# Cross attention in steps: turns four steps behind the scores, keys first in a batch, the projection in two pieces

## The chip, the cores and the metric

The kernel runs on one core of one Trainium2 chip. The metric is the device time of one execution in microseconds (us). The engines are PE (TensorE, with its weight loads shown apart as PEld), DVE (VectorE), ACT (ScalarE), POOL (GpSimd), and SP, which here only issues DMAs.

## What is computed

A gated cross attention with a residual, then a gated feed-forward part of attention with experts. Only the first is touched. There are 32 batches of 100 queries and 361 context rows, 256 channels, and 16 heads of 16 channels.

```python
B, S, _ = q.shape                       # 32, 100, 256; k = v = context: 32, 361, 256
Q = jnp.einsum('bsd,ed->bse', q, Wq) + bq
K = jnp.einsum('bsd,ed->bse', k, Wk) + bk
V = jnp.einsum('bsd,ed->bse', v, Wv) + bv
scores = jnp.einsum('bhqd,bhkd->bhqk', Qm, Km) / jnp.sqrt(jnp.float32(Dh))
scores = jnp.where(attn_mask[:, None, :, :], scores, fill)
attn = jax.nn.softmax(scores, axis=-1)
A = jnp.einsum('bhqk,bhkd->bhqd', attn, Vm)
O = jnp.einsum('bsd,ed->bse', A, Wo) + bo
...
x = x + jnp.tanh(g_xattn[0]) * _L0_xattn_ref(_layernorm(x, axis=-1), ctx_1024, ctx_1024, mask_BxSxS2_bf1, ...)
x = x + jnp.tanh(g_ffn[0]) * _L0_ffn_ref(_layernorm(x, axis=-1), ...)
```

## The kernel before

The kernel has a stage for the queries, one for the cross attention (`stage_cross`), and stages for the experts. In the cross attention the batches follow each other, and each batch is 16 steps, one for each head. Every engine has its own program, written out by hand as a loop over the steps (`body(b)`); there is no scheduler. The engines meet at semaphores alone. Batches 0 and 1 and the last four are written out, the others are a hardware loop of two batches an iteration.

In step i of batch b:

- PE multiplies the scores of head i into one of two banks (`p_s`); this needs the maximum of step i-2 to be taken. Then comes a piece of work for another batch, if the table `ahead` or `behind` has one for this step, then `turn`, which transposes the exponentials of an earlier head (three transposes into one of two banks `p_t`), and in every fourth step `attend`, which multiplies four turned heads with the values into `p_a`.
- DVE (`masked`) adds the mask and takes the minimum over the row, which is the (negated) maximum of the softmax, into one of four buffers `sm`. In ten steps of a batch it also copies a turned head from `p_t` to one of eight buffers `ext`.
- ACT takes the exponentials (`exp`) into one of four buffers `ex`, and copies the other six turned heads (`ACT_COPIES`).

`LAG_T`, `LAG_C`, `LAG_E` and `LAG_A` say by how many steps turns, DVE's copies, ACT's copies and attends stand behind the scores; `lagging` carries them over into the next batch.

```python
def lagging(b, i, lag, work):

    if lag <= i < XH + lag:
        work(b, i - lag)
    elif i < lag and not is_first(b):
        work(b.before(), i - lag + XH)
```

Beside that, each batch needs work for its neighbours. The pieces of `keys` and `values` (three matmuls each, into the two banks `p_p`) make the keys of batch b+2 and the values of batch b+1. ACT and DVE split the keys into two halves of 16 bits (`key_hi`, `key_lo`). SP writes them to `k_parts` in DRAM and reads them back stacked as `c_kst`, once the scores of batch b are done (`stack_keys`). ACT copies the values to `vz`. The context is split by POOL (`split`, a CAST and a subtraction) before keys and values can use it; it waits for the values of the batch that used the buffer before. For the batch behind, DVE inverts the denominators (`invert`), POOL spreads them (`spread`), PE turns them (`turn_rden`), ACT copies them (`copy_rt`), DVE multiplies (`normalize`), PE projects (`project_all`), and DVE adds the residual and takes the moments (`residual`, `moments`, `mean_var`); POOL keeps those (`keep`) and SP stores the batch (`store`).

Of the kernel before, what the change touches and what calls it, by code (L numbers as in the profile page):

```python
# [31 lines left out]
DC = D // P  # L32
XH, XD = 16, 16
XG = P // XD
KC = 3
# [59 lines left out]

def is_last(b):
    return isinstance(b.n, int) and b.n == NB - 1


def later(b, n):  # L100

    if isinstance(b.n, int) and b.n + n >= NB:
        return None
    for _ in range(n):
        b = b.next()
    return b
# [219 lines left out]
def stage_cross(nc, k, sems, queries, cross, x, ctx_t, mask, q_parts, k_parts, big, mv, x1):  # L326
# [7 lines left out]

    LAG_T, LAG_C, LAG_E, LAG_A = 3, 4, 3, 5
    RING = 2 * CLOSE
    RT = 256
    ACT_COPIES = (1, 4, 7, 10, 13, 15)  # L340
# [8 lines left out]
    with ExitStack() as ctx:  # L349
# [46 lines left out]
        def sync_programs(sp):  # L396
            def load_ctx(b):
                at_least(sp, s_cl, b.n - 1)
                sp.dma_start(ctxb[:, b.par, :, :],
                             ctx_t[b.n, :, :].rearrange("(c p) s -> p c s", p=P)  # L400
                             ).then_inc(s_ctx[b.par], 16)
# [51 lines left out]
            def body(b):  # L453
                if not is_last(b):
                    n = b.next()
                    load_queries(n)
                    load_rest(n)
                if later(b, 3):
                    load_ctx(later(b, 3))
                if later(b, 2):  # L460
                    stack_keys(later(b, 2))
                if not is_first(b):
                    store(b.before())

            def rest():
                for g in range(4):
                    sp.wait_ge(queries.s_stored[g], 32)
                batches(sp, body)
                store(fixed(NB - 1))
                for par in range(2):  # L470
                    sp.wait_ge(s_st[par], 16 * NB // 2)
# [3 lines left out]
        def gpsimd(pool):  # L475
# [37 lines left out]
            def body(b):  # L513
                if not is_first(b):
                    spread(b.before())
                bias_x(b)
                if later(b, 1):
                    widen_mask(later(b, 1))
                if later(b, 3):
                    split(later(b, 3))  # L520
                if not is_first(b):
                    keep(b.before())

            widen_mask(fixed(0))
            split(fixed(2))
            pool.wait_ge(s_tg, 1)
            batches(pool, body)
            spread(fixed(NB - 1))
            keep(fixed(NB - 1))

        def vector_programs(dve):
# [64 lines left out]
            def start(n):  # L596
# [5 lines left out]
                elif n == 6:  # L602
# [2 lines left out]
                    dve.tensor_scalar(tgbo[:, :], p_p[:, 0, 0:D], k.tanh_g[:, 0:1], None,  # L605
                                      ALU.mult).then_inc(s_tg, 1)

            def body(b):
                for i in range(XH):
                    lagging(b, i, LAG_C, copy_ext)  # L610
                    masked(b, i)
                    if i == 15 and later(b, 2):
                        key_lo(later(b, 2), 0)
                    if i == 0 and not is_first(b) and later(b, 1):
                        key_lo(later(b, 1), 1)
                    if i == 2 and not is_first(b):
                        invert(b.before())
                    if i == 7 and not is_first(b):
                        normalize(b.before())
                    if i == 11 and not is_first(b):  # L620
                        residual(b.before())
                    if i == 12 and not is_first(b):
                        moments(b.before())
                    if i == 13 and not is_first(b):
                        mean_var(b.before())

            def rest():
                batches(dve, body)
# [11 lines left out]
        def scalar_programs(act):  # L640
# [48 lines left out]
            def body(b):  # L689
                for i in range(XH):  # L690
                    lagging(b, i, LAG_E, copy_ext)
                    if i == 15 and later(b, 2):
                        key_hi(later(b, 2), 0)
                    if i == 0 and not is_first(b) and later(b, 1):
                        key_hi(later(b, 1), 1)
                    if i == 6 and not is_first(b):
                        copy_rt(b.before())
                    if i == 4 and not is_last(b):
                        values(b.next(), 0)
                    exp(b, i)  # L700
                    if i in (6, 9) and not is_last(b):
                        values(b.next(), (4, 6, 9).index(i))

            def rest():
                act.wait_ge(queries.s_zero, 3)
# [8 lines left out]
        def tensor_programs(pe):  # L714
            def keys(b, c, kc):
                if kc == 0:
                    if c == 0:
                        pe.wait_ge(s_cl, b.n + 1)
                    at_least(pe, s_vz, KC * b.n - c)
                for i, (w, x) in enumerate(((whi, ctxh), (whi, ctxl), (wlo, ctxh))):  # L720
                    last = pe.matmul(p_p[:, c, 0:SK], w[:, 0, kc, c * P:(c + 1) * P],
                                     x[:, b.par, kc, :], start=kc == 0 and i == 0,
                                     stop=kc == DC - 1 and i == 2)
                if kc == DC - 1:
                    last.then_inc(s_k, 1)

            def values(b, c, kc):
                if kc == 0:
                    if c == KC - 1:
                        pe.wait_ge(s_vz, KC * b.n + 1)  # L730
                    else:
                        pe.wait_ge(s_klo, DC * b.n + c + 1)
                rows = KW if c < KC - 1 else KL
                for i, (x, w) in enumerate(((ctxh, whi), (ctxh, wlo), (ctxl, whi))):
                    last = pe.matmul(p_p[0:rows, c % 2, 0:D], x[:, b.par, kc, c * KW:c * KW + rows],
                                     w[:, 1, kc, :], start=kc == 0 and i == 0,
                                     stop=kc == DC - 1 and i == 2)
                if kc == DC - 1:
                    last.then_inc(s_v, 1)
# [54 lines left out]
                if c == DC - 1:  # L794
                    last.then_inc(s_o, 1)

            def project_all(b):
                for c in range(DC):
                    project(b, c)

            def start(n):
                if n in (0, 3):
                    for m in range(DC * DC):
# [7 lines left out]
                elif n == 5:  # L811
# [3 lines left out]
                    for c in range(DC):  # L815
# [1 line left out]
                    pe.matmul(p_p[:, 0, 0:D], ones[0:1, :], bor[:, :], start=False,  # L817
                              stop=True).then_inc(s_bo, 1)

            ahead = {1: (1, values, 0, 0), 2: (1, values, 0, 1), 3: (1, values, 1, 0), 5: (1, values, 1, 1),  # L820
                     7: (1, values, 2, 0), 9: (1, values, 2, 1),
                     11: (2, keys, 0, 0), 13: (2, keys, 0, 1), 14: (2, keys, 1, 0), 15: (2, keys, 1, 1)}
            behind = {5: (turn_rden,), 10: (project_all,)}

            def body(b):
                for i in range(XH):
                    scores(b, i)
                    if i in ahead and later(b, ahead[i][0]):
                        n, work, *args = ahead[i]
                        work(later(b, n), *args)  # L830
                    if i in behind and not is_first(b):
                        work, *args = behind[i]
                        work(b.before(), *args)
                    lagging(b, i, LAG_T, turn)
                    lagging(b, i, LAG_A, attend)
# [1018 lines left out]
```

## Time and profile before

| | |
|---|---|
| median of 3 runs | 1934.24 us (1933.02 to 1935.41) |
| the profiled execution | 1932.07 us, span 1930.3 us |
| cross attention, first to last exponential | 69.3 to 584.7 us of the span |
| PE busy over the span | 1871.1 us (97%), weight loads 1145.8 us (59%) |
| DVE, ACT, POOL busy | 1476.6 (76%), 1135.5 (59%), 951.1 us (49%) |

The times are those of single executions; the profile is one of them. Matmuls are pipelined, so the busy time of PE counts more than PE's own work. The span holds stages with different limits, so what this change does has to be read from the stretch of the cross attention. Names such as `c_ps` are the kernel's tiles `p_s` and so on, and L746 is a line of the kernel.

### The profile page before, as it was taken

Reading aid. Unit: us, or ns where it says so; the run is one execution under the profiler, and the core shown is the slowest. Engines: PE = TensorE matmul, PEld = TensorE weight load, DVE = VectorE, ACT = ScalarE, POOL = GpSimd, SP = SyncE. Lnnn points to the kernel's source line nnn. Section 1 sums busy time; section 2 is a strip of 40 time slices with the busy share of each in tenths; the row PEclk is TensorE's granted clock in tenths of the full one; section 3 lists DMA queues with packets and bytes.
Section 4 is the critical chain, followed back from the end, with each engine's and each line's share of the span. In section 5 each row is a group of like instructions: output and inputs, shape, how many; then the busy total and the mean of one; then the engine's idle time right before and its main releaser. Section 6 shows DMA issues by size and latency. Waiting matters only on the chain. (4 is left out here: it accounts for less than half of the span.)

```text
span 1930.3 us, 57615 instructions
## 1 busy us (share of the span) xinstructions
PE 1871.1 (97%) x13454; PEld 1145.8 (59%) x13454; DVE 1476.6 (76%) x4245; ACT 1135.5 (59%) x3591; POOL 951.1 (49%) x1432
## 2 busy tenths in 40 slices
PE   5899999999997999999999999999999999999998
PEld 3688888888875555444444445545555555555543
DVE  6688888888887961555555556658999999999989
ACT  3688888888886444444444445545555555555543
POOL 4022222222212001666666666666677676776766
PEclk9999999999998999999999999999999999999999
DMA  6677888788862484000000023122222222222201
GB/s 156 122 118 117 120 119 120 118 120 119 120 88 88 202 329 188 27 27 27 14 27 27 27 82 97 50 71 66 71 80 67 79 75 72 79 70 76 75 15 64
DMA packets 192148, 174.22 MB, mean 90 GB/s; under 512 B 51921, under 2 KB 183378, under 8 KB 190034
## 3 DMA queue, kind: packets, MB, share of 16 engines
q1 hardware_dynamic: 189906, 165.06, 37.7%
q0 software_dynamic: 2176, 8.39, 1.2%
q8 instruction: 28, 0.46, 0.1%
q14 instruction: 38, 0.31, 0.1%
HBM read 112.41 MB, written 60.98 MB: 90 GB/s over the span
## 5 line engine op out<-in xcount | busy, mean ns | idle before, releaser
L1496 POOL TENSOR_TENSOR o_side<-o_side,o_tmp 128x256 f32 (+1 forms) x528 | 397.2, 752 | 195.8 <-POOL o_side L1496 72.8
L1265 PE MATMUL e_pv<-e_vw,e_xhi 128*128 (+1 forms) x1600 | 475.9, 379 | 1.2 <-ACT e_out L1188 1.2
L1198 ACT ACTIVATE big<-e_pv,gates 128x128 f32<-128x128 f32 x800 | 227.9, 368 | 280.8 <-PE e_pv L1265 279.3
L1624 ACT ACTIVATE o_tmp<-o_py,gates 128x256 f32<-128x256 f32 x528 | 221.8, 473 | 193.0 <-PE o_py L1696 143.8
L661 ACT ACTIVATE c_ex<-c_sm,c_nmax 100x361 f32<-100x361 f32 x512 | 302.1, 592 | 53.5 <-DVE c_nmax L554 46.2
L554 DVE CUSTOM_DVE_ANT_0 c_sm<-c_ps,c_mbias 100x361 f32<-100x361 f32 x512 | 267.4, 523 | 55.9 <-PE c_ps L746 51.2
L1696 PE MATMUL o_py<-o_whi,a_chi 128*128 128x512 f16 x800 | 304.2, 380 | 0.1
L1696 PE MATMUL o_py<-o_wlo,a_chi 128*128 128x512 f16 x800 | 303.8, 380 | 0.0
L1696 PE MATMUL o_py<-o_whi,a_clo 128*128 128x512 f16 x800 | 303.7, 380 | 0.0
L1265 PE MATMUL e_pv<-e_vw,e_xlo 128*128 (+1 forms) x800 | 303.2, 379 | 0.0
L1131 DVE TENSOR_SCALAR e_acc<-e_pv,gates 128x128 f32<-128x128 f32 x400 | 121.8, 346 | 227.5 <-PE e_pv L1265 227.4
L1556 DVE SCALAR_TENSOR_TENSOR o_main<-o_py,gates,o_main 128x256 f32 (+1 forms) x536 | 256.1, 478 | 35.4 <-issue 20.2
L1265 PEld LDWEIGHTS e_pv<-e_vw,e_xhi 128*128 (+1 forms) x1600 | 156.5, 98 | 186.6 <-issue 1.6
L1556 DVE SCALAR_TENSOR_TENSOR o_side<-o_py,gates,o_side 128x256 f32 (+1 forms) x536 | 254.1, 474 | 0.1
L753 PE MATMUL c_pt<-ident,c_ex 100*121 100x100 f32 x1536 | 244.1, 268 | 2.7 <-ACT c_ex L661 0.9
L753 PEld LDWEIGHTS c_pt<-ident,c_ex 100*121 100x121 f32 x1536 | 215.8, 185 | 27.0 <-DVE c_ext L564 7.0
L1014 POOL TENSOR_TENSOR big<-big 128x256 f32<-128x256 f32 x200 | 144.8, 724 | 172.2 <-ACT big L1198 124.1
L493 POOL TENSOR_SCALAR c_mbias<-c_mraw 100x361 f32<-100x361 uint8 x32 | 15.9, 497 | 344.3 <-DMA c_mraw<-in_mask 245.8
L746 PE MATMUL c_ps<-c_kst,c_qst 128*100 128x361 f16 x512 | 172.0, 336 | 5.8 <-DVE c_nmax L554 2.2
L564 DVE COPY c_ext<-c_pt 121x300 f32<-121x300 f32 x320 | 148.5, 464 | 9.3 <-PE c_pt L753 7.5
L1607 ACT ACTIVATE a_ex<-a_ps,a_mxs 100x100 f32<-100x100 f32 x256 | 84.5, 342 | 105.1 <-DVE a_mxs L1527 98.5
L1696 PEld LDWEIGHTS o_py<-o_whi,a_clo 128*128 (+1 forms) x800 | 78.2, 98 | 95.1 <-issue 0.8
(164 smaller groups left out, 3206.4 us busy)
## 6 DMA issues: line engine op xcount, KB each, us to landing
qk<-e_out SPq DMA_DIRECT2D x16, 1600.0 KB, 5.2
c_kst<-k_parts SPq DMA_DIRECT2D x256, 90.2 KB, 4.9
a_q<-qk SPq DMA_DIRECT2D x64, 200.0 KB, 2.4
a_k<-qk SPq DMA_DIRECT2D x64, 200.0 KB, 2.4
v<-e_out SPq DMA_DIRECT2D x20, 640.0 KB, 3.3
a_v<-v SPq DMA_DIRECT2D x64, 200.0 KB
c_ctx<-in_ctx_t SPq DMA_DIRECT2D x32, 361.0 KB, 3.4
e_wst<-in_v_w POOLq DMA_DIRECT2D x8, 1024.0 KB, 7.7
```

The source lines that it names most:

```text
L554: dve.tensor_tensor_reduce(out=sm[:, h % 4, :], in0=p_s[0:SQ, h % 2, 0:SK], in1=mbias[:, b.par, :], scale=-0.25 / WS, scalar=BIG, op0=ALU. ...
L564: dve.tensor_copy(ext[:, h % RING, :], p_t[0:KW, h % 2, 0:KC * SQ]).then_inc(s_extd, 1)
L661: act.activation(ex[:, h % 4, 0:SK], sm[:, h % 4, :], ACT.Exp, scale=-1.0, bias=nmax[:, h % 4:h % 4 + 1], accum_out=den[:, b.par, HEAD[h]: ...
L746: pe.matmul(p_s[0:SQ, h % 2, 0:SK], qst[:, b.par, HEAD[h], :], kst[:, b.par, HEAD[h] // 2, :], start=True, stop=True).then_inc(s_s, 1)
L753: last = pe.transpose(p_t[0:KW, h % 2, c * SQ:(c + 1) * SQ], ex[:, h % 4, c * KW:(c + 1) * KW], k.ident[0:SQ, 0:SQ])
L1014: pool.tensor_tensor(tsum[:, hh, :, :], tmp[:, hh, 0:2, :], tmp[:, hh, 2:4, :], ALU.add).then_inc(s_ts, 1)
L1198: act.activation(tmp[:, hh, e, :], p_v[:, hh, 1, e * PD:(e + 1) * PD], ACT.Copy, scale=gate).then_inc(s_av, 1)
L1265: last = pe.matmul(p_v[:, hh, half, :], a[:, c, bass.ds(t * P, P)], vw[:, bass.ds(col + (w * DC + c) * VW, 512)], start=j == 0, stop=j == ...
L1496: pool.tensor_tensor(side[:, x.t, :], side[:, x.t, :], tmp[:, slot(x, r), j, :], ALU.add).then_inc(s_pool, 1)
L1556: dve.scalar_tensor_tensor(out=into[:, x.t, :], in0=p_y[:, q, j, :], scalar=gate, in1=into[:, x.t, :], op0=ALU.mult, op1=ALU.add).then_inc ...
L1624: act.activation(tmp[:, slot(x, r), j, :], p_y[:, q, j, :], ACT.Copy, scale=gate).then_inc(s_av, 1)
L1696: last = pe.matmul(p_y[:, q, :, :].rearrange("p j d -> p (j d)"), a[:, bass.ds(buf * T + x.t * P, P)], b[:, buf, cut], start=j == 0, stop= ...
```

## The change

All four lags grow by one, so turns, copies and attends stand one step further behind the scores. The keys of batch b+2 are made in steps 0, 2, 3 and 4 instead of 11, 13, 14 and 15; the values of batch b+1 in steps 6, 7, 8, 10, 11 and 12 instead of 1, 2, 3, 5, 7 and 9. Attends now stand in steps 1, 5, 9 and 13, where no other piece stands. The projection is split over steps 14 and 15 instead of being whole in step 10, and the residual, moments, `keep` and `store` of a batch follow it, two batches behind, at the start of the next. In the last batch the projection stands in steps 11 and 12. ACT's and DVE's shares of the keys and values move with them.

```diff
--- before.py
+++ after.py
@@ -95,6 +95,10 @@
 
 def is_last(b):
     return isinstance(b.n, int) and b.n == NB - 1
+
+
+def has_two_before(b):
+    return not isinstance(b.n, int) or b.n >= 2
 
 
 def later(b, n):
@@ -334,7 +338,7 @@
 
 
 
-    LAG_T, LAG_C, LAG_E, LAG_A = 3, 4, 3, 5
+    LAG_T, LAG_C, LAG_E, LAG_A = 4, 5, 4, 6
     RING = 2 * CLOSE
     RT = 256
     ACT_COPIES = (1, 4, 7, 10, 13, 15)
@@ -457,15 +461,16 @@
                     load_rest(n)
                 if later(b, 3):
                     load_ctx(later(b, 3))
+                if has_two_before(b):
+                    store(b.before().before())
                 if later(b, 2):
                     stack_keys(later(b, 2))
-                if not is_first(b):
-                    store(b.before())
 
             def rest():
                 for g in range(4):
                     sp.wait_ge(queries.s_stored[g], 32)
                 batches(sp, body)
+                store(fixed(NB - 2))
                 store(fixed(NB - 1))
                 for par in range(2):
                     sp.wait_ge(s_st[par], 16 * NB // 2)
@@ -518,14 +523,15 @@
                     widen_mask(later(b, 1))
                 if later(b, 3):
                     split(later(b, 3))
-                if not is_first(b):
-                    keep(b.before())
+                if has_two_before(b):
+                    keep(b.before().before())
 
             widen_mask(fixed(0))
             split(fixed(2))
             pool.wait_ge(s_tg, 1)
             batches(pool, body)
             spread(fixed(NB - 1))
+            keep(fixed(NB - 2))
             keep(fixed(NB - 1))
 
         def vector_programs(dve):
@@ -605,24 +611,28 @@
                     dve.tensor_scalar(tgbo[:, :], p_p[:, 0, 0:D], k.tanh_g[:, 0:1], None,
                                       ALU.mult).then_inc(s_tg, 1)
 
+            def tail(b, step):
+                if step == 0:
+                    residual(b)
+                if step == 1:
+                    moments(b)
+                if step == 2:
+                    mean_var(b)
+
             def body(b):
                 for i in range(XH):
                     lagging(b, i, LAG_C, copy_ext)
                     masked(b, i)
-                    if i == 15 and later(b, 2):
-                        key_lo(later(b, 2), 0)
-                    if i == 0 and not is_first(b) and later(b, 1):
-                        key_lo(later(b, 1), 1)
+                    if i in (3, 5) and later(b, 2):
+                        key_lo(later(b, 2), i // 5)
                     if i == 2 and not is_first(b):
                         invert(b.before())
-                    if i == 7 and not is_first(b):
+                    if i == 9 and not is_first(b):
                         normalize(b.before())
-                    if i == 11 and not is_first(b):
-                        residual(b.before())
-                    if i == 12 and not is_first(b):
-                        moments(b.before())
-                    if i == 13 and not is_first(b):
-                        mean_var(b.before())
+                    if has_two_before(b):
+                        tail(b.before().before(), i)
+                    if is_last(b):
+                        tail(b.before(), i - 12)
 
             def rest():
                 batches(dve, body)
@@ -689,17 +699,13 @@
             def body(b):
                 for i in range(XH):
                     lagging(b, i, LAG_E, copy_ext)
-                    if i == 15 and later(b, 2):
-                        key_hi(later(b, 2), 0)
-                    if i == 0 and not is_first(b) and later(b, 1):
-                        key_hi(later(b, 1), 1)
-                    if i == 6 and not is_first(b):
+                    if i in (2, 4) and later(b, 2):
+                        key_hi(later(b, 2), i // 4)
+                    if i == 7 and not is_first(b):
                         copy_rt(b.before())
-                    if i == 4 and not is_last(b):
-                        values(b.next(), 0)
+                    if i in (8, 11, 14) and not is_last(b):
+                        values(b.next(), (8, 11, 14).index(i))
                     exp(b, i)
-                    if i in (6, 9) and not is_last(b):
-                        values(b.next(), (4, 6, 9).index(i))
 
             def rest():
                 act.wait_ge(queries.s_zero, 3)
@@ -716,7 +722,8 @@
                 if kc == 0:
                     if c == 0:
                         pe.wait_ge(s_cl, b.n + 1)
-                    at_least(pe, s_vz, KC * b.n - c)
+                    done = b.n if isinstance(b.n, int) and b.n < 2 else b.n - 1
+                    at_least(pe, s_vz, KC * done - c)
                 for i, (w, x) in enumerate(((whi, ctxh), (whi, ctxl), (wlo, ctxh))):
                     last = pe.matmul(p_p[:, c, 0:SK], w[:, 0, kc, c * P:(c + 1) * P],
                                      x[:, b.par, kc, :], start=kc == 0 and i == 0,
@@ -728,8 +735,11 @@
                 if kc == 0:
                     if c == KC - 1:
                         pe.wait_ge(s_vz, KC * b.n + 1)
+                    elif is_last(b):
+                        pe.wait_ge(s_vz, KC * b.n)
                     else:
-                        pe.wait_ge(s_klo, DC * b.n + c + 1)
+                        keyed = b.n if is_first(b) else b.n + 1
+                        pe.wait_ge(s_klo, DC * keyed + c + 1)
                 rows = KW if c < KC - 1 else KL
                 for i, (x, w) in enumerate(((ctxh, whi), (ctxh, wlo), (ctxl, whi))):
                     last = pe.matmul(p_p[0:rows, c % 2, 0:D], x[:, b.par, kc, c * KW:c * KW + rows],
@@ -794,10 +804,6 @@
                 if c == DC - 1:
                     last.then_inc(s_o, 1)
 
-            def project_all(b):
-                for c in range(DC):
-                    project(b, c)
-
             def start(n):
                 if n in (0, 3):
                     for m in range(DC * DC):
@@ -817,10 +823,10 @@
                     pe.matmul(p_p[:, 0, 0:D], ones[0:1, :], bor[:, :], start=False,
                               stop=True).then_inc(s_bo, 1)
 
-            ahead = {1: (1, values, 0, 0), 2: (1, values, 0, 1), 3: (1, values, 1, 0), 5: (1, values, 1, 1),
-                     7: (1, values, 2, 0), 9: (1, values, 2, 1),
-                     11: (2, keys, 0, 0), 13: (2, keys, 0, 1), 14: (2, keys, 1, 0), 15: (2, keys, 1, 1)}
-            behind = {5: (turn_rden,), 10: (project_all,)}
+            ahead = {0: (2, keys, 0, 0), 2: (2, keys, 0, 1), 3: (2, keys, 1, 0), 4: (2, keys, 1, 1),
+                     6: (1, values, 0, 0), 7: (1, values, 0, 1), 8: (1, values, 1, 0), 10: (1, values, 1, 1), 11: (1, values, 2, 0), 12: (1, values, 2, 1)}
+            behind = {6: (turn_rden,), 14: (project, 0), 15: (project, 1)}
+            behind_last = {6: (turn_rden,), 11: (project, 0), 12: (project, 1)}
 
             def body(b):
                 for i in range(XH):
@@ -828,8 +834,9 @@
                     if i in ahead and later(b, ahead[i][0]):
                         n, work, *args = ahead[i]
                         work(later(b, n), *args)
-                    if i in behind and not is_first(b):
-                        work, *args = behind[i]
+                    owed = behind_last if is_last(b) else behind
+                    if i in owed and not is_first(b):
+                        work, *args = owed[i]
                         work(b.before(), *args)
                     lagging(b, i, LAG_T, turn)
                     lagging(b, i, LAG_A, attend)
```

**The projection on PE.** The first place is a batch of the loop, steps 10 and 11 before, on PE. L746 is the scores, L792 the projection, L753 a turn, and `c_s_sm`, `c_s_an`, `c_s_ex`, `c_s_extd` are the semaphores of the maxima, of `normalize`, of the exponentials and of DVE's copies. Before:

```order
L746 MATMUL c_ps<-c_kst,c_qst 100x361 [waits c_s_sm]
L792 MATMUL c_pa<-c_w,c_an 100x256 [waits c_s_an]
L792 MATMUL c_pa<-c_w,c_an 100x256
L393 REGISTER_ALU [waits c_s_ex]
L753 MATMUL c_pt<-ident,c_ex 121x100 [waits c_s_extd]
L753 MATMUL c_pt<-ident,c_ex 121x100 x2
```

After, the same matmuls stand in steps 14 and 15, here L756, L802 and L763:

```order
L756 MATMUL c_ps<-c_kst,c_qst 100x361 [waits c_s_sm]
L802 MATMUL c_pa<-c_w,c_an 100x256 [waits c_s_an]
L397 REGISTER_ALU [waits c_s_ex]
L763 MATMUL c_pt<-ident,c_ex 121x100 [waits c_s_extd]
L763 MATMUL c_pt<-ident,c_ex 121x100 x2
L53 REGISTER_ALU
L756 MATMUL c_ps<-c_kst,c_qst 100x361 [waits c_s_sm]
L802 MATMUL c_pa<-c_w,c_an 100x256
```

One half of the projection now stands in each of two steps, with a turn and scores between the halves.

**The start of a batch on PE.** The second place is the first step of the loop, after its branch. Before, scores, a turn and an attend (L774):

```order
L53 ISA [waits c_s_qst_0,c_s_kst_0]
L746 MATMUL c_ps<-c_kst,c_qst 100x361 [waits c_s_sm]
L750 ISA
L393 ISA [waits c_s_ex]
L753 MATMUL c_pt<-ident,c_ex 121x100 [waits c_s_extd]
L753 MATMUL c_pt<-ident,c_ex 121x100 x2
L391 ISA [waits c_s_extd]
L774 MATMUL c_pa<-c_ext,c_v 32x100 [waits c_s_exta]
L774 MATMUL c_pa<-c_ext,c_v 32x100 x11
```

After, a piece of keys (L728) stands between scores and turn, with its waits for the split of the context (`c_s_cl`) and for ACT's copies of the values (`c_s_vz`), and the attend stands behind the next scores:

```order
L53 ISA [waits c_s_qst_0,c_s_kst_0]
L756 MATMUL c_ps<-c_kst,c_qst 100x361 [waits c_s_sm]
L724 REGISTER_ALU
L53 ISA [waits c_s_cl]
L728 MATMUL c_pp<-c_ctxhi,c_whi 128x361 [waits c_s_vz]
L728 MATMUL c_pp<-c_ctxlo,c_whi 128x361
L728 MATMUL c_pp<-c_ctxhi,c_wlo 128x361
L760 ISA
L395 ISA [waits c_s_ex]
L763 MATMUL c_pt<-ident,c_ex 121x100 [waits c_s_exta]
L763 MATMUL c_pt<-ident,c_ex 121x100 x2
L756 MATMUL c_ps<-c_kst,c_qst 100x361 [waits c_s_sm]
```

The keys were in step 11 before, with the same two waits.

**The third values copy on ACT.** The third place is ACT in the same batch of the loop. L652 is the copy of the third piece of values, L686 a copy of ext, L661 an exponential. Before, it stands between the exponential of step 9 and the ext copy of step 10:

```order
L650 REGISTER_ALU
L652 ACTIVATE c_v<-c_pp 119x8x2x16
L686 ACTIVATE c_ext<-c_pt 121x300
L659 REGISTER_ALU
L661 ACTIVATE c_ex,c_den<-c_sm,c_nmax 100x361
L659 REGISTER_ALU
L661 ACTIVATE c_ex,c_den<-c_sm,c_nmax 100x361
L659 REGISTER_ALU
L661 ACTIVATE c_ex,c_den<-c_sm,c_nmax 100x361
```

After (L662, L696, L671), it stands behind the ext copy of step 14, with two exponentials left in the batch:

```order
L671 ACTIVATE c_ex,c_den<-c_sm,c_nmax 100x361
L696 ACTIVATE c_ext<-c_pt 121x300
L660 REGISTER_ALU
L662 ACTIVATE c_v<-c_pp 119x8x2x16
L669 REGISTER_ALU
L671 ACTIVATE c_ex,c_den<-c_sm,c_nmax 100x361
L669 REGISTER_ALU
L671 ACTIVATE c_ex,c_den<-c_sm,c_nmax 100x361
```

It moved by five steps, and what waits for its bank is now the piece of keys at the start of the next batch.

## Rows read from the trace of the kernel before

**Rows 1.** Busy us: PE, PEld, DVE, ACT, POOL; clock, DMA share, GB/s.

```profile
148.64:520.10 371.46, 370.41 (x4510) 311.24 (x4509) 320.59 (x1128) 321.92 (x1013) 92.52 (x137) 1.00 0.82 120
```

**Rows 2.** Timeline of PE, scores matmuls alone: start, duration (us), what.

```profile
81.63 0.32 PE L746 MATMUL c_ps<-c_kst,c_qst 128*100 128x361 f16 x1
...
148.64 0.32 PE L746 MATMUL c_ps<-c_kst,c_qst 128*100 128x361 f16 x1
...
331.80 0.36 PE L746 MATMUL c_ps<-c_kst,c_qst 128*100 128x361 f16 x1
...
332.81 0.32 PE L746 MATMUL c_ps<-c_kst,c_qst 128*100 128x361 f16 x1
...
333.26 0.32 PE L746 MATMUL c_ps<-c_kst,c_qst 128*100 128x361 f16 x1
...
334.07 0.36 PE L746 MATMUL c_ps<-c_kst,c_qst 128*100 128x361 f16 x1
...
335.60 0.36 PE L746 MATMUL c_ps<-c_kst,c_qst 128*100 128x361 f16 x1
...
336.42 0.32 PE L746 MATMUL c_ps<-c_kst,c_qst 128*100 128x361 f16 x1
...
337.73 0.32 PE L746 MATMUL c_ps<-c_kst,c_qst 128*100 128x361 f16 x1
...
338.65 0.32 PE L746 MATMUL c_ps<-c_kst,c_qst 128*100 128x361 f16 x1
...
339.85 0.36 PE L746 MATMUL c_ps<-c_kst,c_qst 128*100 128x361 f16 x1
...
346.45 0.36 PE L746 MATMUL c_ps<-c_kst,c_qst 128*100 128x361 f16 x1
...
347.87 0.36 PE L746 MATMUL c_ps<-c_kst,c_qst 128*100 128x361 f16 x1
...
520.10 0.32 PE L746 MATMUL c_ps<-c_kst,c_qst 128*100 128x361 f16 x1
```

**Rows 3.** Timeline of PE, DVE and weight loads (PEld), steps 6 to 8.

```profile
332.97 0.46 PE L753 MATMUL c_pt<-ident,c_ex 100*121 100x100 f32 x3
...
333.10 0.47 DVE L564 COPY c_ext<-c_pt 121x300 f32<-121x300 f32 x1 [0.18 <-PE c_pt L753]
...
333.49 0.52 DVE L554 CUSTOM_DVE_ANT_0 c_sm<-c_ps,c_mbias 100x361 f32<-100x361 f32 x1
...
333.93 0.47 DVE L564 COPY c_ext<-c_pt 121x300 f32<-121x300 f32 x1
...
334.45 0.39 PEld L753 LDWEIGHTS c_pt<-ident,c_ex 100*121 100x121 f32 x3 [0.26 <-DVE c_ext L564]
```

**Rows 4.** Waits from 100 to 580 us: total us, times, longest.

```profile
DVE c_sm L554 <- PE c_ps L746: 48.4, 91, 0.7
```

**Rows 5.** Groups of DVE, 100 to 580 us: busy us, mean ns, idle before.

```profile
L543 DVE SCALAR_TENSOR_TENSOR c_klo<-c_pp,c_bk,c_khi 128x361 f16<-128x361 f32 x57 | 33.8, 594 | 9.5 <-ACT c_khi L644 9.2
...
L580 DVE SCALAR_TENSOR_TENSOR big<-c_pa,tanh_g,c_xbias 100x256 f32 (+1 forms) x29 | 13.9, 479 | 0.0
```

**Rows 6.** Timeline of ACT: a copy of ext, then one of values.

```profile
331.67 0.40 ACT L686 ACTIVATE c_ext<-c_pt 121x300 f32<-121x300 f32 x1
332.10 0.38 ACT L652 ACTIVATE c_v<-c_pp 121x256 f32<-121x256 f32 x1
```

**Rows 7.** Timeline of SP's queue (SPq, time to issue) and POOL.

```profile
330.46 3.66 SPq L432 DMA_DIRECT2D c_kst<-k_parts  x8
...
335.35 3.75 SPq L410 DMA_DIRECT2D c_qst<-q_parts  x8
...
340.40 0.40 SPq L399 DMA_DIRECT2D c_ctx<-in_ctx_t  x1
...
344.02 0.79 POOL L480 CAST c_ctxhi<-c_ctx 128x722 f16<-128x722 f32 x1 [1.07 <-DMA c_ctx<-in_ctx_t]
344.89 1.57 POOL L482 TENSOR_TENSOR c_ctxlo<-c_ctx,c_ctxhi 128x722 f16<-128x722 f32 x1
```

## The prediction, made before the changed kernel was run

> **What bounds the kernel now.** I read the stretch table first. Between 148.64 and 520.10 us, which is 23 batches from the scores of batch 5 to those of batch 28, one batch takes 371.46 / 23 = 16.15 us [rows 1, 2]. In that stretch the PE row says busy for 370.41 of 371.46 us; DVE has 320.59 (13.94 a batch), ACT 321.92 (14.00 a batch), the clock is at its upper level (1.00 of 2.4 GHz), and the DMA engines are busy for 0.82 of the time.
>
> Busy time doesn't say how full PE is, since the next matmul starts before the one ahead of it ends. So I took the starts of the scores matmuls, one for each step of a batch, and read a step's length as the distance to the next start [rows 2]. Step 5 starts at 331.80. The step with nothing but scores and a turn (6) takes 333.26 - 332.81 = 0.45. With a piece of values it takes 0.82 (steps 7 and 9), with a piece of keys 0.92 (step 11), with an attend 1.20 (step 12), with values and the turn of the denominators 1.01 (step 5), with the whole projection 1.31 (step 10). These lengths are the shortest of their kind, and I take them as PE's own work. But step 8, also an attend step, takes 1.53, and step 4 of the next batch 1.42, where step 12 takes 1.20.
>
> One batch of PE's own work is 5 x 0.82 + 4 x 0.92 + 4 x 1.20 + 1.01 + 0.46 + 1.32 = 15.37 us. The batch takes 16.15, so **0.78 us a batch is idle time of PE**: 0.33 in step 8, 0.22 in step 4, the rest in small pieces around the start of a batch. Over 32 batches that is 25 us, and no reordering that leaves PE's work as it is gives back more in the steady part.
>
> Step 8 shows what the wait is [rows 3]. The turn of step 5 ends at about 0.17 after the scores of step 6 (as the one at 332.97 does: 333.43 against 333.26). DVE then copies it (333.10), takes the maximum of step 6 (333.49), and copies the turn of step 6 (333.93 to 334.40). PE's turn in step 8 needs that second copy, and its weight load starts at 334.45, idle for 0.26, released by the copy. So the loop is DVE's: copy, maximum, copy take 0.39 + 0.44 + 0.47, about 1.3 us, while PE passes through step 6 (0.45) and step 7 (0.81) and stands at the turn of step 8. It arises because the bare step 6 is followed by a short one and then an attend step, whose turn comes right behind the scores. The waits table agrees from the other side: DVE waits 48.4 us in 91 places for scores, behind PE's long steps [rows 4]. PE's load is uneven: DVE starves in the long steps and is late after the short ones.
>
> **The change, part by part.** *Work.* Nothing is removed or added: same matmuls, copies, DMAs. The sum stays 15.37: the projection becomes two steps of 0.46 + 0.43 = 0.89 in place of one of 1.32 and one bare step.
>
> *PE's steps after.* In order from 0: keys 0.92, attend 1.20, keys 0.92, 0.92, 0.92, attend 1.20, values with the denominators 1.01, values 0.82, 0.82, attend 1.20, values 0.82, 0.82, 0.82, attend 1.20, projection 0.89, 0.89. No bare step is left; the steps ahead of the attend steps 9 and 13 are values of 0.82. For step 9, redo the sum of [rows 3]: the turn of step 6 ends 0.17 after scores 7, the copy starts 0.05 later, and copy, maximum, copy end at 0.22 + 1.30 + 0.05 = 1.57. PE reaches the load of that turn at 0.82 + 0.82 + 0.03 = 1.67. The wait of 0.33 is gone with 0.1 to spare. In the attend steps 1 and 5 the steps ahead are of 0.92, so there is more. I cost these at nothing; the gain is 0.33 + 0.22 + the small ones.
>
> *Turns four steps behind.* Turn, copies and attends all move by one step against the scores, so each copy keeps its distance to the turn that waits for it. The only new closeness is that ex has four buffers: exp of step i needs the turn of step i-4, now issued in the same step. That turn ends 0.17 after the next scores, 1.1 us after its own in a keys step; exp can't start sooner than scores 0.32 + 0.22 + maximum 0.53 + 0.05 = 1.12 anyway. No cost.
>
> *DVE's load.* Residual (0.48), moments (the same input, taken as long) and both key_lo (0.59 each) now fall into steps 0 to 5 [rows 5]. Each next start comes about 0.08 before an end, as in [rows 3], so they take 0.40 x 2 + 0.51 x 2 = 1.82, and with invert and mean_var (half a residual each, my estimate for their small tiles) 2.22. With 6 maxima of 0.44 and 4 copies of 0.39 that is 6.42, against PE's 6.08 in these steps. DVE ends 0.34 behind; the room is that the maximum of step i must end before scores i+2, that is 1.84 at least against 1.12. So 0.7 of room, half of it used, and steps 6 to 9 give it back. In return DVE no longer waits for key_hi.
>
> *A new wait: keys in step 0.* PE's first keys piece writes the bank that ACT's third values copy reads. ACT now does that copy in step 14, behind the copy of ext (the order of ACT, above). The ext copy starts 0.22 after scores 15, the values copy 0.43 later and it lasts 0.38 [rows 6]: done at 1.03, released at 1.08 after scores 15. Scores 0 start 0.89 after scores 15. So PE, which reaches the keys' weight load at once, is released 0.19 late; normally the matmul follows scores by 0.16, now load and matmul by 0.19 + 0.10: **0.1 us a batch** lost (I take 0.1; from 0 to 0.3). Behind it on PE stand turn and attend, which have room.
>
> *SP and POOL.* SP issues kst of batch b+1 once the scores of batch b-1 are done and, so far, once the keys arrive at the start of b. With the keys a batch earlier only the first holds it. Now the chain runs from kst at 330.46 to ctx at 340.40, the CAST of ctx starts at 344.02: 13.56 us. Of the 1.23 between the end of the kst issues and the first of q, where the store of x1 stands now, I take 0.9 away, since it moves behind ctx [rows 7]. So ctx is there 12.7 after kst. kst is issued when scores 15 end, 0.5 before the batch, so ctx lands at 12.2. The CAST also waits for values, whose last piece now ends in step 12, at 12.3. With 0.87 to the next start and 1.57 for the subtraction the split is done at 14.8, and the keys of step 0 need it at 15.4: 0.6 to spare. Queries and mask come 4 us sooner than now, far from the maximum that needs them. No cost, but this is the thinnest cover in the change.
>
> *Sum.* A steady batch takes 15.37 + 0.10 = 15.47, 0.68 less. 23 batches: 15.6. The four from 81.63 to 148.64 take 16.75 each; 0.68 x 4 = 2.7, and a little of their surplus, 0.3. Batches 28 to 30: 0.68 + 0.68 + 0.4 = 1.7; the drain has one turn and copy more, -0.4. In all 19.9 us. The profiled execution took 1932.07 us (span 1930.3); it becomes 1912.2. The median of the runs is 2.2 above it, so I forecast 1914.
>
> **What a page says of the PE row.** PE's busy row gives 99.7%, and taken as occupancy it leaves 1 us in the stretch and no gain at all. The Trainium skill, Perfetto Trace Analysis, Identifying the Most-Contended Engine, says that matmul busy time is no good measure, since matmuls are pipelined, and that weight-load busy time should be read instead; by that, 311.24 of 371.46 (84%), an estimate would leave up to 60 us. The starts of scores leave 18 of the stretch, between the two, and the sum goes by them.
>
> **Rivals.** *R1, part of the waits stays* (0.20). ACT and DVE are both at 14 of what would be 15.5 us, 90%; the 0.1 at step 9 or ACT's three pairs of copies, ext then values, are missed by a little in several steps. For: my margins are of 0.1. Against: each was worked out with rows of this very order of work. Half the gain: 1924. *R2, nothing comes of it* (0.08): PE's short lengths can't be had back to back, or each wait moves to the next step: 1934. For: the PE row. Against: 1.53 and 1.20 for the same work in one batch. *R3, slower* (0.07): PE waits in step 0 for the split of the context. It becomes a loss once ctx lands more than 0.6 + 0.7 = 1.3 us later than I work out, since each batch then pays more than 0.68. 2 us late: (1.4 - 0.68) x 28 = +20, 1954. For: DMA busy share 0.82 now, 0.86 in a shorter batch, and all transfers bunched in its first part. Against: the sum of transfers is the same, and the batch holds 0.6 of slack. *R4, better* (0.03): no wait in step 0 and the start's surplus gone: 0.78 x 32 + 3 = 28, 1906. My forecast, 1908 to 1921, has 0.62.
>
> **Numbers.** This kernel's runs lie within 0.12%, and 0.2% (3.9 us) is about what can be told from no change. Faster: 0.62 + 0.20 + 0.03 = 0.85; same 0.08; slower 0.07. The range goes from R4's 1906 to 1928, on R1's side; left out are R3, most of R2 and the slow end of R1.
>
> **What would show it.** Right: distances of scores of 0.82, 0.92, 1.20 and 0.89 all through a batch and 15.4 to 15.6 us a batch; step 9 at 1.20; a keys load in step 0 released by ACT's values copy; DVE's wait for scores below 48 us; kst issued just ahead of scores 0. Wrong: batches of 15.8 or more with idle time before a turn, released by ext copies (R1), or before the first keys load, released by ctxlo (R3).

## The result, and the profile after

The changed kernel takes 1911.21 us (median of 4 runs, 1909.45 to 1914.11) against 1933.72 before: a ratio of 0.9884, 95% interval 0.9868 to 0.9899. The forecast was 1914. Its profiled execution has a span of 1909.4 us, 20.9 less than before. The ratios further down are each against runs of the kernel before taken beside that run, with medians of 1931.6 to 1932.3; lengths of steps and batches are read from one profiled execution of each kernel.

The busy row of the 23 batches 5 to 27 of the changed kernel (columns as in [rows 1]):

```profile
149.02:505.68 356.66, 353.48 (x4510) 305.90 (x4509) 323.30 (x1128) 318.87 (x1014) 93.19 (x138) 1.00 0.90 124
```

A batch takes 356.66 / 23 = 15.51 us, where it took 16.15. Then PE's timeline, scores alone: steps 6 to 9 of batch 26, and from its step 15 steps 15 and 0.

```profile
480.64 0.36 PE L756 MATMUL c_ps<-c_kst,c_qst 128*100 128x361 f16 x1
...
481.66 0.32 PE L756 MATMUL c_ps<-c_kst,c_qst 128*100 128x361 f16 x1
...
482.44 0.32 PE L756 MATMUL c_ps<-c_kst,c_qst 128*100 128x361 f16 x1
...
483.22 0.32 PE L756 MATMUL c_ps<-c_kst,c_qst 128*100 128x361 f16 x1
...
484.44 0.36 PE L756 MATMUL c_ps<-c_kst,c_qst 128*100 128x361 f16 x1
...
488.95 0.32 PE L756 MATMUL c_ps<-c_kst,c_qst 128*100 128x361 f16 x1
...
489.84 0.32 PE L756 MATMUL c_ps<-c_kst,c_qst 128*100 128x361 f16 x1
...
491.30 0.32 PE L756 MATMUL c_ps<-c_kst,c_qst 128*100 128x361 f16 x1
```

Step 6 takes 1.02, steps 7 and 8 0.78 each, and the attend step 9 takes 1.22, where the attend step 8 took 1.53 in [rows 2]. Step 15, with half of the projection, takes 0.89. But step 0 of batch 27 takes 1.46 us; the same step of batch 26 takes 0.91. All even batches of the steady part take 15.29 us, and the odd ones 15.3 to 16.4, the excess being in step 0. Two things can hold up the first keys piece there: ACT's third values copy, which has to leave the bank, and POOL's split of the context. The waits table (total us, times, longest), 100 to 565 us:

```profile
DVE c_sm L560 <- PE c_ps L756: 29.4, 106, 0.6
...
PEld c_pp L728 <- ACT c_v L662: 5.3, 10, 0.8
...
PE c_pp L728 <- POOL c_ctxlo L487: 4.4, 7, 1.5
```

The first line is DVE's wait for scores, 48.4 us before. The table gives most of the waits of the keys piece to ACT's values copy. The timelines of PEld, ACT and POOL at the step of 1.46 say otherwise:

```profile
489.47 0.38 ACT L662 ACTIVATE c_v<-c_pp 119x256 f32<-119x256 f32 x1
...
487.98 0.78 POOL L485 CAST c_ctxhi<-c_ctx 128x722 f16<-128x722 f32 x1 [1.62 <-DMA c_ctx<-in_ctx_t]
488.85 1.56 POOL L487 TENSOR_TENSOR c_ctxlo<-c_ctx,c_ctxhi 128x722 f16<-128x722 f32 x1
...
490.53 0.10 PEld L728 LDWEIGHTS c_pp<-c_ctxhi,c_whi 128*128 128x128 f16 x1 [0.65 <-ACT c_v L662]
```

The values copy ends at 489.85, 0.01 after scores 0 and 0.68 before the load that it is said to have released. The split of the context ends at 490.41, 0.12 before the load. PE waits for the context.

### The profile page after: what moved, and what is told of

Its sections match the earlier page's. It is cut to its first block and busy times, and to the rows that moved or that the text cites. A ratio compares the mean times of both kernels' runs of the same rounds, so it can differ in the third digit from the quotient of the medians.

```text
span 1909.4 us, 57667 instructions
## 1 busy us (share of the span) xinstructions
PE 1851.2 (97%) x13454; PEld 1140.5 (60%) x13454; DVE 1480.2 (78%) x4245; ACT 1132.8 (59%) x3591; POOL 951.3 (50%) x1432
## 5 line engine op out<-in xcount | busy, mean ns | idle before, releaser
L671 ACT ACTIVATE c_ex<-c_sm,c_nmax 100x361 f32<-100x361 f32 x512 | 302.3, 594 | 40.3 <-DVE c_nmax L560 19.3
L763 PE MATMUL c_pt<-ident,c_ex 100*121 100x100 f32 x1536 | 238.1, 264 | 1.8 <-DVE c_ext L570 1.1
L763 PEld LDWEIGHTS c_pt<-ident,c_ex 100*121 100x121 f32 x1536 | 219.8, 186 | 16.7 <-issue 2.5
L756 PE MATMUL c_ps<-c_kst,c_qst 128*100 128x361 f16 x512 | 168.5, 329 | 1.5 <-DVE c_nmax L560 1.2
L1272 PEld LDWEIGHTS e_pv<-e_vw,e_xlo 128*128 (+1 forms) x800 | 78.3, 98 | 94.3
```

What stands on the lines that cost most here:

```text
L671: act.activation(ex[:, h % 4, 0:SK], sm[:, h % 4, :], ACT.Exp, scale=-1.0, bias=nmax[:, h % 4:h % 4 + 1], accum_out=den[:, b.par, HEAD[h]: ...
L756: pe.matmul(p_s[0:SQ, h % 2, 0:SK], qst[:, b.par, HEAD[h], :], kst[:, b.par, HEAD[h] // 2, :], start=True, stop=True).then_inc(s_s, 1)
L763: last = pe.transpose(p_t[0:KW, h % 2, c * SQ:(c + 1) * SQ], ex[:, h % 4, c * KW:(c + 1) * KW], k.ident[0:SQ, 0:SQ])
L1272: last = pe.matmul(p_v[:, hh, half, :], a[:, c, bass.ds(t * P, P)], vw[:, bass.ds(col + (w * DC + c) * VW, 512)], start=j == 0, stop=j == ...
```

## Where the 20.9 us come from

By the starts of the scores in the two traces, in us saved: batch 0 0.4; batches 1 to 4 -0.9; the 23 batches 14.8; batches 28 to 30 4.4; batch 31 0.6; the first scores 0.1 earlier; from the last scores to the last mean_var -1.3 (8.1 before, 9.4 after). The rest, 2.7, comes after the cross attention, in stages that the change doesn't touch; the eleven profiled executions here take 1334.0 to 1338.8 us for them, the kernel before the longest, and I don't count it as the change's. That leaves 18.2 us for the cross attention.

## Experiments

Theory A: PE's uneven steps, with DVE's loop behind them, cost the time; B: it is the distance between exponential and turn; C: it is the DMAs, which come earlier when keys come first.

**e1_lags_only.** Kernel before, with the edit below; ACT's copy of the turned denominators moves from step 6 to 7, and DVE's multiplication from step 7 to 9.

```diff
-    LAG_T, LAG_C, LAG_E, LAG_A = 3, 4, 3, 5
+    LAG_T, LAG_C, LAG_E, LAG_A = 4, 5, 4, 6
...
-            behind = {5: (turn_rden,), 10: (project_all,)}
+            behind = {6: (turn_rden,), 10: (project_all,)}
```

> The kernel before with the four lags one greater and nothing else of the change, except that the turn of the denominators, its copy and the multiplication stand one, one and two steps later, since the last attend of a batch now stands in step 5. Theory A (the gain is evenness of PE's steps: no bare step ahead of an attend step, so DVE's loop of copy, maximum, copy is never late): lags alone bring nothing, since attends now share steps 1, 5, 9 and 13 with values or keys (1.56 to 1.66 us) and steps 0, 4, 8 and 12 are bare (0.46 us); a batch stays at 16.1 us or grows, time 1933 or more. Theory B (the gain is the greater distance between exponential and turn): half of the gain or more is here, a batch of 15.8 us or less, 1924 or less.

Measured: 1957.5 us, ratio 1.0135 (1.0118 to 1.0152), 17.11 us a batch. The greater distance alone brings nothing, but it came with new waits, so this run by itself doesn't exclude B. What does is the waits table of the kernel before, 100 to 580 us: the weight loads of turns wait for an exponential once, for 0.6 us, and for DVE's copies 26 times, 6.8 us in all. B falls by that. The loss here is larger than bare steps explain. The turn of step 7 waits 0.5 us in each batch for a copy of ACT, and step 1, with attend and values, takes 2.60 us, since step 0 is bare and PE comes to the values too early. The weight load of the values waits for the low half of the keys, which DVE takes from the bank at the start of the batch:

```profile
271.05 0.13 PEld L735 LDWEIGHTS c_pp<-c_whi,c_ctxhi 128*121 128x121 f16 x1 [0.92 <-DVE c_klo L543]
```

**e2_lags_back.** The changed kernel with the four lags at 3, 4, 3, 5.

> The changed kernel with the four lags of before, so attends share steps 0, 4, 8 and 12 with keys or values. Theory A: uneven steps again (1.66, then 0.46 in steps 1, 5, 9, 13 apart from the denominators), so waits of 0.2 to 0.4 us at several turns: a batch of 15.8 to 16.2 us, 1918 to 1930. Theory C (the gain comes from the DMAs that now arrive earlier, because keys come first in a batch): nothing is lost, 1911 within 2.

Measured: 1924.0 us, 0.9959 (0.9945 to 0.9973), 15.93 us a batch. As A expects: turns wait for DVE's copies again, in steps 3, 7 and 11, each two steps behind a bare one. This line of the waits table, 152 to 518 us, has no counterpart in the same stretch of the changed kernel:

```profile
PEld c_pt L763 <- DVE c_ext L570: 6.2, 35, 0.2
```

Here the DMAs are as early as in the changed kernel, and 0.22 of the 0.64 us is there, so C has at most a third of it by itself. **e9_ctx_first_lags_back** has the same lags in the kernel of e4 below:

> The kernel of e4_ctx_first with the lags of before: the price of the lags with no wait for the context beside it. From e2, where the context wasn't waited for in the steady part, a batch takes 15.92 us against e4's 15.29, which is 0.63 x 23 = 14.5 us in the steady part and some 4 in the other batches: 1917 to 1921. If part of e2's loss was a DMA or the context after all, it is less than 1914.

Measured: 1919.2 us, 0.9940 (0.9923 to 0.9956), 15.93 us again. So the lags are worth 0.64 us a batch in this table of work, and cost 1 us in the old one (17.11 against 16.15).

**e3_step6_filled.** Kernel before, the bare step filled:

```diff
-            ahead = {1: (1, values, 0, 0), 2: (1, values, 0, 1), 3: (1, values, 1, 0), 5: (1, values, 1, 1),
+            ahead = {1: (1, values, 0, 0), 2: (1, values, 0, 1), 3: (1, values, 1, 0), 6: (1, values, 1, 1),
```

> The kernel before with one piece of values moved from step 5 to step 6, which was bare; nothing else. Theory A: the wait of 0.33 us at the turn of step 8 goes, a batch takes 15.8 to 15.9 us, 1923 to 1927. Theories B and C: lags and DMAs are as before, so no change, 1933.

Measured: 1929.1 us, 0.9987 (0.9975 to 0.9999), 16.01 us a batch, short of the 1923 to 1927 that A gave. Steps 8 of the 23 batches fall from 1.53 to 1.28 us on average, as DVE's loop asks. But step 15 grows from 0.98 to 1.19: the next scores wait for their queries. The waits table of e3, 148 to 516 us, has it where it could name the DMA:

```profile
PE c_ps L746 <- DMA c_qst<-q_parts: 1.9, 5, 0.5
```

That wait was in the kernel before too; this is its scores of batch 4:

```profile
131.87 0.35 PE L746 MATMUL c_ps<-c_kst,c_qst 128*100 128x361 f16 x1 [0.29 <-DMA c_qst<-q_parts]
```

**e7_step6_store_late.** e3 with the store of x1 out of SP's chain from keys to queries.

> e3_step6_filled with SP's store of x1 moved ahead of the keys' stacking, out of the chain keys, kst, store, queries. In e3 step 8 fell by 0.25 us but step 15 grew by 0.21, with PE waiting for the queries' DMA. If that chain is the second bound, taking 0.5 to 0.9 us out of it gives step 15 back: 15.8 us a batch, 1922 to 1925. If step 15 grew for another reason (the wait moves along PE whatever the DMAs do), nothing changes: 16.0 us a batch, 1929 within 2.

Measured: 1928.1 us, 0.9983 (0.9973 to 0.9992), 16.00 us a batch. SP issues the queries 0.6 us earlier: on average over batches 6 to 27 they start 4.07 us after the first issue of kst, against 4.68 in e3. But the last of them lands 11.57 us after it in both. The expectation of 15.8 is refuted: the start of the issue isn't the limit.

**e8_half_queries.** e3 with half of the queries' loads, so half of each score's terms are left out:

```diff
-                for ab in range(2):
+                for ab in range(1):
...
-                    pe.wait_ge(s_qst[b.par], 128 * (b.half + 1))
+                    pe.wait_ge(s_qst[b.par], 64 * (b.half + 1))
```

> e3_step6_filled with only four of the eight loads of queries in each batch (the other half of the stacked queries stays zero, so half of each score's terms are left out; all else is computed as before). In e3 and in e7 the queries land 0.24 us before the scores that wait for them, though e7 issues them 0.6 us earlier. If the DMA engines' own work (kst, then queries) is the bound there and not SP's issue, half of the queries land 1 us or more earlier, step 15 falls from 1.19 to 0.92, a batch takes 15.8 us and the time is 1921 to 1925. If PE's wait in step 15 has another cause, a batch stays at 16.0 us and the time at 1929 within 2.

Measured: 1920.6 us, 0.9945 (0.9929 to 0.9962), 15.85 us a batch, step 15 at 0.92 in every batch. The queries now land 10.85 us after the first issue of kst, 0.7 us sooner and not the 1 us or more expected. So the queries' DMAs were a second bound, hardly behind the first. That it is the transfers' own time is likely but not isolated: four loads also take SP 1.8 us to issue instead of 3.7, and e7 moved the start of the issue only.

**e4_ctx_first.** The changed kernel with SP's order

```diff
+                if later(b, 3):
+                    load_ctx(later(b, 3))
                 if not is_last(b):
                     n = b.next()
-                    load_queries(n)
                     load_rest(n)
-                if later(b, 3):
-                    load_ctx(later(b, 3))
+                    load_queries(n)
```

> The changed kernel with SP's loads in another order: context, mask and x before the queries, instead of the queries first and the context last. If what is left of waits in step 0 is the split of the context that comes late (ctx lands 12.0 to 13.7 us into a batch), every batch takes 15.29 us, the wait of 3.1 us in batch 1 goes too, and the time falls by 9 to 12 us to 1900 to 1902. If it is ACT's copy of the values, as the waits table says (5.3 us of it), step 0 stays as it is: 1911 within 2, with 15.5 us a batch.

Measured: **1900.4 us, 0.9839 (0.9823 to 0.9856)**, the shortest time here. SP also increments a semaphore of its own behind two of its waits, as it did behind others. The busy row and POOL's timeline:

```profile
141.65:493.38 351.73, 351.73 (x4510) 306.65 (x4509) 322.49 (x1128) 317.70 (x1014) 93.36 (x138) 1.00 0.90 126
```

```profile
475.11 0.79 POOL L487 CAST c_ctxhi<-c_ctx 128x722 f16<-128x722 f32 x1 [1.63 <-PE c_pp L747]
475.99 1.56 POOL L489 TENSOR_TENSOR c_ctxlo<-c_ctx,c_ctxhi 128x722 f16<-128x722 f32 x1
```

351.73 / 23 = 15.29 us, the same for every batch from 2 to 27. The CAST is now released by PE's values, not by the DMA, and the split ends 0.54 before scores 0. Batches 1 to 4 give 6.7 us back: in the changed kernel the first keys load of batch 1 waits 3.21 us for the split and step 0 takes 4.76 us, in e4 1.02. In that batch the wait costs more than itself: step 1 takes 2.03 us against 1.20, and the clock granted to PE is 0.50 to 0.56 of 2.4 GHz from 84.4 to 87.9 us, its lower level, after 1.00 before the idle time.

**e6_ctx_late.** The changed kernel with the context's load behind the store of x1.

> The changed kernel with the load of the context behind the store of x1 on SP, so it is issued some 0.5 us later; nothing else. If the split of the context is what PE waits for in step 0, the odd batches pay the whole delay and the even ones, which have 0.3 us of room, the rest: 0.3 to 0.4 us a batch, 15.8 to 15.9 us, and 1920 to 1924. If the wait is for ACT's copy of the values, nothing changes: 1911 within 2.

Measured: 1917.5 us, 0.9913 (0.9893 to 0.9932), 15.74 us a batch. The sign is that of the context, but the dose isn't: batch 5 alone pays 4.0 us more than in the changed kernel (its first keys load waits 2.5 us, with the split done 0.1 us before it, and its steps 1 and 2 take 1.94 and 1.77 instead of 1.20 and 0.95, with a granted clock of 0.56 and 0.52 there), the other 22 together 1.4 us, and even batches nothing. So the slower clock is part of what batch 5 pays, and the dose can't be read as a straight price of delay; e4 carries the verdict.

**e5_whole_projection.** e4 with the projection whole:

```diff
-            behind = {6: (turn_rden,), 14: (project, 0), 15: (project, 1)}
+            behind = {6: (turn_rden,), 14: (project_all,)}
```

> The kernel of e4_ctx_first with the projection whole in step 14, so step 14 should take 1.32 us and step 15, bare, 0.46. If the split in two steps matters, it does so through a wait that the even steps cover: ACT's third values copy ends 0.90 us after scores 15 (scores 0 now come at 0.89, then at 0.46), so the first keys piece waits about 0.4 to 0.5 us in step 0, a batch takes 15.7 to 15.8 us and the time is 1913 to 1917. If only the place of the projection matters and not its split, a batch stays at 15.29 us and the time at 1900 within 2.

Measured: 1910.7 us, 0.9890 (0.9873 to 0.9906), 15.65 us a batch, somewhat less than expected: 0.35 more than e4, in step 0, by the wait that was expected. Here the releaser named is the right one, since the copy ends 0.45 after the start of scores 0:

```profile
268.65 0.10 PEld L730 LDWEIGHTS c_pp<-c_ctxhi,c_whi 128*128 128x128 f16 x1 [0.45 <-ACT c_v L664]
```

## Why the prediction was right, step by step

- *PE's own work, 15.37 us*: right to 0.08. e4 shows 15.29. A values step takes 0.78, and 0.82 only right behind an attend step; step 7 of [rows 2] was 0.03 above its shortest.
- *The waits of steps 8 and 4 go*: right. In e4 all 16 steps are at the shortest seen, but for step 9 with 1.22 against 1.20, so the margin of 0.1 there was all but used up. e3 shows the loop by itself.
- *Turns four steps behind*: no cost, right; but I costed them at no gain either, only as a shift. e9 shows 0.64 us a batch. What I left out is that the lag decides which steps hold the attends. With the old one they share steps with keys and values, 1.56 to 1.70 us and then a bare step of 0.49. The sum of each such pair is no longer than before; the loss comes two steps behind the bare one, where steps 7 and 11 take 1.04 and 1.00 instead of 0.78, 0.48 of the 0.64.
- *A new wait, keys in step 0, 0.1 us*: the term was mis-sized. ACT's copy ends 0.90 after scores 15, not 1.03, and costs nothing. e5 shows what it costs once the cover of 0.43 us is gone.
- *SP and POOL, no cost, 0.6 to spare*: wrong, and the largest miss in the mechanism. R3's mechanism takes 0.22 us a batch, 5 us in the steady part, and in batch 1 4.7 us (3.9 in step 0, 0.8 in step 1). The term that failed is the 0.9 us taken off for the store of x1. SP does issue the context 0.6 us earlier, 9.08 us after the first issue of kst against 9.68 before, averaged over batches 6 to 27. But it lands after 13.15 us against 13.03, and in e7, where the store alone moved, after 12.95. In the batches that pay, the CAST starts 13.83 us after kst, where I had 12.7. Hence 4.61 from the context's issue to the CAST (487.98) and not 3.62: the issue moved, the landing didn't. (The DMA engines were busy for 0.90 of the time, where I had 0.86.) Of the gap between kst and queries 0.65 also stayed in even batches (474.01 + 3.65 to 478.31):

```profile
474.01 3.65 SPq L436 DMA_DIRECT2D c_kst<-k_parts  x8
478.31 3.74 SPq L414 DMA_DIRECT2D c_qst<-q_parts  x8
...
483.37 0.40 SPq L403 DMA_DIRECT2D c_ctx<-in_ctx_t  x1
484.13 0.32 SPq L441 DMA_DIRECT2D x<-big  x1
484.56 0.40 SPq L427 DMA_DIRECT2D k_parts<-c_khi  x1
485.01 0.47 SPq L427 DMA_DIRECT2D k_parts<-c_klo  x1
```

  Behind the context now come the store and the writes of the keys; before, SP issued nothing for 4 us there. In the batches that pay, the landing is 0.4 us later than in the kernel before (13.59 against 13.20). That these transfers cause it is an argument, not shown.
- *Queries and mask come earlier, no gain*: incomplete. e3, e7 and e8 show that the queries' DMAs were a second bound near 16.0 us a batch. So evenness would hardly have given 0.64 us without the keys moved ahead; no run has the even steps with the old DMAs.
- *The sum*: steady part 14.8 against 15.6; batches 1 to 4 -0.9 against 3.0; batches 28 to 30 4.4 against 1.7; batches 0 and 31, for which the sum had nothing, 1.0; drain -1.3 against -0.4. The stage gave 18.2 of the 19.9 us forecast. That the total agrees so well is luck in part: the misses at both ends of the stage partly cancel (batches 28 to 30 took 16.56, 17.42 and 15.70 before, more than the steady batch that I reckoned with), and 2.7 us of the 20.9 come from stages that the change doesn't touch.
- *The page on PE's busy row*: the row says 100% in e4, with every step at its shortest, and said 99.7% before, with 5% idle: it is no measure, as the Trainium skill, Perfetto Trace Analysis, Identifying the Most-Contended Engine, says. The page names two measures instead, MFU (the share of peak arithmetic) and weight-load busy time, and I used the second alone. It is 306.65 of 351.73 (87%) in e4, so the 60 us that I drew from it before were not there; that the rest up to 100% is room was my reading, not the page's. The starts of one recurring instruction gave the size.

## What to carry to other kernels

Where one engine is near full, write down its work a step by the starts of an instruction that recurs in each step, take the shortest length of each kind, and look where steps of the same work differ. Fill bare steps, above all ahead of one whose result is waited for at once. When work moves ahead by a batch, follow every transfer that it needs to its landing, with the transfers now issued behind it, and issue the one with the least room first: here that was worth 9 to 12 us on top of the change's 22 (9.0 with each kernel against its own runs of the kernel before, 10.8 by the medians, 11.9 by the profiled executions). An earlier issue is not yet an earlier landing: read the landing from the trace. A releaser named in a table has to be checked against the end times of all that the instruction waits for.

## What the runs showed that I had not expected

The queries land no earlier when issued 0.6 us earlier (e7, with the DMA engines 0.89 busy), while half as many are no longer waited for (e8): the order and amount of transfers counted, and a start of the issue 0.6 us earlier didn't. The same holds for the context in the changed kernel, and that was the prediction's hole. And a small move far from the bound can cost more than the change gains: e1, four numbers and the places of three operations, took 26 us more.
